# A third exact block in Q's projection, with the engines' orders around it rearranged, in a decoder layer on one core

## The chip, the cores and the metric

One core of one Trainium2 chip runs the whole program. The metric is device time of one execution, in microseconds. Both kernels are timed on the same chip.

## The reference

Three blocks follow each other on x of 2 x 512 rows and 1024 columns, each with a LayerNorm in front and a residual sum behind:

```python
x = x + attn(layernorm(x), q_codes, q_scales, ...)   # 32 heads of 128, 8 K/V heads, rotary, causal
x = x + matmul(fake_quant(layernorm(x)), fake_quant(ctx))   # ctx 2 x 1024 x 1024, codes 0..255
x = x + einsum('bsi,oi->bso', layernorm(x), bw)      # bw = mean|w| * sign(w) - clip(w) + clip(w)
```

The attention's four weight matrices are 4-bit codes with a float scale for each 128 input rows and each output column:

```python
w = codes.astype(float32) - 8.0
w = w * repeat(scales, 128, axis=0)
q = hidden @ w_q        # 1024 x 4096; K and V 1024 x 1024; O 4096 x 1024
```

## The kernel before

**Products.** A float32 product is made of float16 halves: upper by upper, upper by lower and lower by upper, three matmuls of TensorE (`three_products`). Where a factor is a code it is exact in float16, and two matmuls do.

**Slots.** After LayerNorm, V and K, the attention runs over 64 slots (p = 0 to 63). A slot is one head h and one batch b: eight groups g of eight slots i, h = i // 2, b = i % 2. Groups 1 to 4 (slots 8 to 39) are a hardware loop and also handle the cross attention's context (`with_ctx`). Slots 0 to 6 and 40 to 63 carry units of the feed-forward weight: an early part (clip, sign, difference, sum) and a late part (upper and lower half, turned by DMA). Work of several tiles overlaps in a slot p: scores and softmax of p, the weighing of V (`weigh`) of p - 1, the O projection of earlier heads in four units (`o_unit`, `o_add`), and Q of p + 2 (`Q_AHEAD`).

**Q.** Q^T of a tile has eight blocks of 128 input rows. From the fifth tile on (`by_parts`) the first `N_EXACT` = 2 of them use the codes themselves. `q_exact(0)` multiplies block 0, two matmuls, into the bank `q_ps`; ScalarE then multiplies the bank by the ratio of the scales of blocks 0 and 1 (`q_base(0)`, L1313); `q_exact(1)` adds block 1; `q_base(1)` brings the sum to block 1's scale; `q_part` adds the other six blocks by three products each, with weights whose scale was multiplied in beforehand. The ratios are computed once in seven small steps on VectorE (`ratio_step`), one in each of the K phase's rounds x = 4 to 10, and put into columns of `o_table`.

**Pieces.** Weights arrive in pieces of 512 columns, one a slot. VectorE multiplies codes by scales (`piece_scale`, L1894), ScalarE writes the upper half (`piece`, L1215, L1216), VectorE the lower (`piece_lo`, L1900). In even slots the first 256 columns of a piece are exact ones: ScalarE copies the codes, VectorE skips them. In odd slots all 512 are scaled.

**Rotation.** ScalarE copies the finished Q (`q_copy`) and swaps its halves (`q_swap`), GpSimd multiplies by cosine and sine (`q_turn`, `sine`), VectorE adds (`q_sum`, L2054), ScalarE writes the upper half (`q_hi`, L1321), GpSimd the lower (`q_lo`, L1707).

**Softmax.** The scores' 128-row blocks come in three units, `SCORE_UNITS = [[(3, 0)], [(2, 0), (0, 384)], [(1, 0)]]`: widths 512; 384 and 128; 256. VectorE takes the maxima (`maxima`, L2141), ScalarE the exponentials with their sums (`exps`, L1346), VectorE the reciprocals (L2224 for units 0 and 1, L2232 for unit 2), GpSimd normalises (`norm`, L1687), ScalarE and GpSimd split into halves (L1373, L1694), DMA turns them, TensorE weighs (`weigh`, L949) into the bank `pv_ps`, the second of `side_ps`. `ao_part` (ScalarE) and `ao_rest` (VectorE) split that.

**Order.** Every engine's order in a slot is written by hand in its `slot` function, with semaphores between engines. TensorE's is: scores 0, `q_exact(0)`, O unit 3 of the slot before, scores 1, `q_exact(1)`, O unit 0, scores 2, `q_part`, O units 1 and 2, weigh. A bank of O is free when VectorE's `o_add` of the unit two before is done.

**Feed-forward unit.** GpSimd clips 128x256 weights (`wf_clip`), ScalarE takes the sign (`wf_sign`, L1408), VectorE forms mean times sign less clipped (`wf_difference`, L2101), GpSimd adds the clipped again (`wf_add`); one slot later ScalarE and VectorE split into halves (L1415, `wf_lower` L2107).

## Time and profile before

| | |
|---|---|
| median of 3 runs | 1050.31 us (1050.2 to 1050.74) |
| the profiled execution | 1050.22 us, span 1048.4 us |
| TensorE, VectorE, ScalarE, GpSimd busy in the span | 97%, 86%, 74%, 75% |
| granted TensorE clock | 1.00 |
| distance from one slot's start to the next, slots 8 to 61 | 11.46 us |

The span is from the first to the last instruction. Busy time counts an instruction's whole record, and on TensorE records of neighbouring matmuls overlap, so 100% there says that matmuls follow each other without a gap. In a timeline each line is one instruction or several like ones: its start, its length, its engine and source line, and in brackets how long the engine stood idle before it and what ended that. A slot starts with the first 512-column matmul of the scores.

### The profile page before, as it was taken

Reading aid. Unit: us, or ns where it says so; the run is one execution under the profiler, and the core shown is the slowest. Engines: PE = TensorE matmul, PEld = TensorE weight load, DVE = VectorE, ACT = ScalarE, POOL = GpSimd, SP = SyncE. Lnnn points to the kernel's source line nnn. Section 1 sums busy time; section 2 is a strip of 40 time slices with the busy share of each in tenths; the row PEclk is TensorE's granted clock in tenths of the full one; section 3 lists DMA queues with packets and bytes.
Section 4 is the critical chain, followed back from the end, with each engine's and each line's share of the span. In section 5 each row is a group of like instructions: output and inputs, shape, how many; then the busy total and the mean of one; then the engine's idle time right before and its main releaser. Section 6 shows DMA issues by size and latency. Waiting matters only on the chain.

```text
span 1048.4 us, 18487 instructions
## 1 busy us (share of the span) xinstructions
PE 1015.7 (97%) x5296; PEld 500.5 (48%) x5296; DVE 902.7 (86%) x1651; ACT 774.4 (74%) x1712; POOL 788.9 (75%) x833
## 2 busy tenths in 40 slices
PE   5999998999999999999999999999999999989998
PEld 3444343445555555555555455545555554454443
DVE  7989997699888888888888889999999998887773
ACT  5547766888898888888888888888888887473210
POOL 3678787899878887887888789999999999332200
PEclk9999999999999999999999999999999999999999
DMA  9783301676887676667667766777787765534442
GB/s 337 258 199 121 116 26 34 145 152 157 161 162 166 138 165 158 147 152 159 165 138 165 157 147 140 153 165 150 156 150 156 160 138 113 118 122 96 88 96 74
DMA packets 309804, 152.01 MB, mean 145 GB/s; under 512 B 257728, under 2 KB 274240, under 8 KB 309728
## 3 DMA queue, kind: packets, MB, share of 16 engines
q1 hardware_dynamic: 301952, 137.76, 58.0%
q10 hardware_dynamic: 7776, 13.37, 4.5%
q8 instruction: 31, 0.51, 0.2%
q14 instruction: 45, 0.37, 0.1%
HBM read 85.26 MB, written 4.19 MB: 85 GB/s over the span
## 4 chain that ended last, share of the span: by engine, by line
PE 82%; DVE 6%; POOL 5%; ACT 3%; issue 2%; DMA 1%; ACTq 0%; SPq 0%; DVEq 0%; POOLq 0%
PE out_ps L969 10%; PE proj_ps L969 9%; PE side_ps L949 9%; PE side_ps L757 8%; PE side_ps L759 8%; PE side_ps L758 8%; PE side_ps L845 5%; PE proj_ps L1130 5%; PE score_ps L932 3%; PE score_ps L933 3%; PE score_ps L934 3%; PE proj_ps L1135 2%; PE score_ps L1100 2%; PE out_ps L780 1%; PE proj_ps L757 1%
## 5 line engine op out<-in xcount | busy, mean ns | idle before, releaser
L1687 POOL TENSOR_SCALAR prob<-prob,row_inv 128x512 f32<-128x512 f32 (+3 forms) x256 | 196.7, 779 | 81.9 <-DVE row_inv L2224 80.3
L1694 POOL TENSOR_TENSOR w_b<-prob,w_b 128x896 f16<-128x896 f32 (+2 forms) x192 | 186.0, 995 | 6.5 <-ACT w_b L1373 6.4
L1346 ACT ACTIVATE prob<-score_ps,neg_max 128x512 f32<-128x512 f32 (+3 forms) x256 | 132.9, 526 | 30.7 <-DVE neg_max L2141 29.1
L2154 DVE SCALAR_TENSOR_TENSOR x_acc<-out_ps,o_now,x_acc 128x1024 f32<-128x1024 f32 x120 | 153.1, 1276 | 1.3 <-PE out_ps L969 1.3
L2154 DVE SCALAR_TENSOR_TENSOR x_acc<-proj_ps,o_now,x_acc 128x1024 f32<-128x1024 f32 x120 | 153.0, 1275 | 0.0
L757 PE MATMUL side_ps<-hT,w_a 128*128 128x512 f16 x384 | 145.5, 379 | 0.5 <-ACT side_ps L1313 0.2
L759 PE MATMUL side_ps<-hT,w_a 128*128 128x512 f16 x384 | 145.5, 379 | 0.0
L758 PE MATMUL side_ps<-hT,w_a 128*128 128x512 f16 x384 | 145.5, 379 | 0.0
L2141 DVE CUSTOM_DVE_ANT_0 score_ps<-score_ps,mask_b 128x512 f32<-128x512 f32 (+3 forms) x256 | 122.7, 501 | 16.9 <-PE score_ps L934 16.6
L969 PE MATMUL proj_ps<-work,w_b 128*128 128x512 f16 x496 | 127.3, 379 | 1.9 <-DVE x_acc L2154 1.5
L969 PE MATMUL out_ps<-work,w_b 128*128 128x512 f16 x496 | 127.3, 379 | 0.8 <-DVE x_acc L2154 0.7
L949 PE MATMUL side_ps<-work,v_sb 128*128 128x512 f16 (+3 forms) x768 | 114.8, 299 | 0.2 <-DMA work<-w_b 0.2
L1900 DVE SCALAR_TENSOR_TENSOR w_a<-stage_s,w_a 128x256 f16<-128x256 f32 (+1 forms) x64 | 64.7, 1010 | 43.4 <-ACT w_a L1216 43.1
L1373 ACT ACTIVATE w_b<-prob 128x896 f16<-128x896 f32 (+2 forms) x192 | 99.3, 550 | 3.6 <-POOL prob L1687 1.6
L1313 ACT ACTIVATE side_ps<-side_ps,o_now 128x512 f32<-128x512 f32 x120 | 79.3, 661 | 27.8 <-PE side_ps L845 24.3
L1682 POOL TENSOR_TENSOR swapped<-swapped,sin_t 128x512 f32<-128x512 f32 x77 | 99.7, 1295 | 0.0
L949 PEld LDWEIGHTS side_ps<-work,v_sb 128*128 128x128 f16 (+1 forms) x768 | 69.6, 98 | 45.3 <-DMA work<-w_b 1.2
L932 PE MATMUL score_ps<-k_sb,q_sb 128*128 (+4 forms) x256 | 76.7, 299 | 3.6 <-ACT prob L1346 2.0
L1707 POOL TENSOR_TENSOR q_sb<-rot,q_sb 128x512 f16<-128x512 f32 x62 | 78.9, 1273 | 0.0
L969 PEld LDWEIGHTS proj_ps<-work,w_b 128*128 128x128 f16 x496 | 48.2, 98 | 60.2 <-DVE x_acc L2154 2.5
L969 PEld LDWEIGHTS out_ps<-work,w_b 128*128 128x128 f16 x496 | 48.3, 98 | 59.7 <-DVE x_acc L2154 2.0
L933 PE MATMUL score_ps<-k_sb,q_sb 128*128 (+4 forms) x256 | 76.6, 299 | 0.0
(276 smaller groups left out, 2230.1 us busy)
## 6 DMA issues: line engine op xcount, KB each, us to landing
stage_c<-in_codes_dram SPq DMA_DIRECT2D x72, 256.0 KB, 2.9
stage_o<-in_codes_dram SPq DMA_DIRECT2D x64, 256.0 KB, 3.3
stage_s<-in_scales_dram SPq DMA_DIRECT2D x34, 256.0 KB, 3.7
ctx_raw<-in_ctx_dram ACTq DMA_DIRECT2D x32, 256.0 KB, 3.2
work<-w_b SPq DMA_TRANSPOSE x261, 3.1
x_acc<-in_x_dram SPq DMA_DIRECT2D x8, 512.0 KB, 8.9
k_sb<-in_codes_dram SPq DMA_DIRECT2D x16, 256.0 KB, 7.0
v_sb<-in_scales_dram SPq DMA_DIRECT2D x16, 256.0 KB, 7.4
```

The lines of the kernel that those rows point to most:

```text
L757: pe.matmul(o, stat(0), mov(0), start=first, stop=False, skip_group_check=onto)
L758: pe.matmul(o, stat(0), mov(1), start=False, stop=False, skip_group_check=onto)
L759: return pe.matmul(o, stat(1), mov(0), start=False, stop=last, skip_group_check=onto)
L932: pe.matmul(o, q[0], k[0], start=True, stop=False)
L933: pe.matmul(o, q[0], k[1], start=False, stop=False)
L949: mm = pe.matmul(pv_ps[:, kb * P:S], v_sb[:, bass.ds(g, 1), l, b * TB + kb, :].rearrange("p a d -> p (a d)"), probT[:, m, at:kb + (TB - 1) ...
L969: mm = pe.matmul(o[:, b, :], o_codes[:, h % RING, cb * P:(cb + 1) * P], ao[:, h % 2, l, b * S:(b + 1) * S], start=l == 0, stop=l == 1)
L1346: ins = act.activation(prob[:, SCORE_AT[qb]:SCORE_AT[qb] + w], score_ps[:, score_bank(i, u), off:off + w], ACT.Exp, bias=neg_max[:, c:c + ...
L1687: return pool.tensor_scalar(prob[:, at:at + w], prob[:, at:at + w], row_inv[:, col:col + 1], P_UP, ALU.mult, ALU.mult)
L1694: ins = pool.tensor_tensor(prob16[:, 1, to:to + w], prob[:, at:at + w], prob16[:, 0, to:to + w], ALU.subtract)
L2141: ins = dve.tensor_tensor_reduce(s, s, mask_b[:, S - w:S], -1.0, MAX_FROM, ALU.add, ALU.min, neg_max[:, c:c + 1])
L2154: ins = dve.scalar_tensor_tensor(y, u, s, y, ALU.mult, ALU.add)
```

## The change

`N_EXACT` goes from 2 to 3. What goes with it:

- TensorE: `q_exact(2)`, two matmuls, stands for the third block's three. The unit of scores with two blocks is cut in two parts; `q_exact(1)` comes between them, `q_exact(2)` behind O unit 0, and O unit 1 moves ahead of scores 2.
- ScalarE: `q_base(1)` moves ahead of the first exponentials, `q_base(2)` is new behind them, O's codes are cut behind it, Q's upper half moves ahead of the third exponentials. The second conversion of the context's codes (128x512, 8-bit codes to bfloat16) leaves ScalarE for VectorE. K's late swap and upper half move to the ends of slots 1 and 2.
- VectorE: Q's sum moves ahead of the third maxima. O's first add stands ahead of that sum in slots without context and behind the first reciprocal in slots with context, where the conversion follows the second reciprocal. The late K steps move behind the feed-forward difference. In even slots `piece_scale` and `piece_lo` skip 384 columns, not 256.
- The ratios take ten steps and not seven; `q_ratio` has two rows per head and lies in the end of `ctx_raw`.
- For feed-forward units 8 to 29 the sign goes to `pv_ps` and the difference reads it there. ScalarE waits for the attention output of two slots before to have left the bank, and `weigh` waits for the difference.

```diff
-N_EXACT = 2
+N_EXACT = 3
+RATIO_STEPS = 3 * N_EXACT + 1
+        def in_psum(u):
+            return KB <= u < WF_UNITS - 2
+        def wf_sign_place(u):
+            return pv_ps[:, 0:WF_W] if in_psum(u) else wf_place(u)[1]
# TensorE, weigh
                 pe.wait_ge(prob_turned, p * TURNED + TURNED)
+                if known(p) and WF_FROM <= p + 1 and in_psum(wf_early(p + 1) or 0):
+                    pe.wait_ge(wf_diff, wf_early(p + 1) + 1)
# TensorE, slot
-                first_o = known(p) and p == O_LAG
-                if has_o and not first_o:
+                if known(p) and p == O_LAG:
+                    o_unit(p, i, 0)
+                elif has_o:
                     o_unit(p - 1, prev[1], 3)
-                scores(p, i, g, 1)
-                if first_o:
-                    o_unit(p, i, 0)
-                    o_unit(p, i, 1)
+                scores(p, i, g, 1, slice(0, 1))
                 if has_ahead and parts:
                     q_exact(*ahead, 1)
+                scores(p, i, g, 1, slice(1, 2))
...
-                if has_o and not first_o:
-                    o_unit(p, i, 0)
+                if has_o:
+                    o_unit(p, i, int(known(p) and p == O_LAG))
+                if has_ahead and parts:
+                    q_exact(*ahead, 2)
                 if has_ahead and not parts:
                     q_part(*ahead, range(0, 1))
+                if has_o and not (known(p) and p == O_LAG):
+                    o_unit(p, i, 1)
                 scores(p, i, g, 2)
...
-                    if not first_o:
-                        o_unit(p, i, 1)
                     o_unit(p, i, 2)
# ScalarE, wf_sign
-                if u >= 2:
+                if in_psum(u):
+                    act.wait_ge(ao_ready, WF_FROM + u - KB - 1)
+                elif u >= 2:
                     act.wait_ge(wf_split, u)
-                act.activation(diff, raw, ACT.Sign).then_inc(wf_signed, 1)
+                act.activation(wf_sign_place(u), wf_place(u)[0], ACT.Sign).then_inc(wf_signed, 1)
# ScalarE, slot
                     q_base(*next_q, 0)
-                if known(p) and p == 1:
-                    late_swaps()
-                if known(p) and p == 2:
-                    late_upper()
+                if has_ahead and by_parts(p + Q_AHEAD):
+                    q_base(*next_q, 1)
                 exps(p, i, 0)
                 if has_ahead and by_parts(p + Q_AHEAD):
-                    q_base(*next_q, 1)
+                    q_base(*next_q, 2)
+                o_cut(p, i)
                 if has_next and not by_parts(p + 1):
                     q_hi(p + 1)
-                o_cut(p, i)
                 exps(p, i, 1)
+                if has_next and by_parts(p + 1):
+                    q_hi(p + 1)
...
                 exps(p, i, 2)
+                if known(p) and p == 1:
+                    late_swaps()
+                if known(p) and p == 2:
+                    late_upper()
...
-                if has_next and by_parts(p + 1):
-                    q_hi(p + 1)
-                if with_ctx:
-                    act.wait_ge(ctx_scaled, q + 1)
-                    act.activation(dst, ctx_codes, ACT.Copy, bias=-Q_MID).then_inc(ctx_free, 1)
# VectorE, slot
                 maxima(p, i, 1)
+                if not with_ctx:
+                    first_add()
+                if has_next and by_parts(p + 1):
+                    q_sum(p + 1)
                 maxima(p, i, 2)
-                if has_o:
-                    if i % B:
-                        dve.wait_ge(o_now_ready, g * RF + i // B)
-                    o_add(p, i, 0)
                 dve.wait_ge(exp_done, p * 3 + 2)
                 dve.reciprocal(row_inv[:, 0:3], row_sum[:, 0:3]).then_inc(inv_ready[0], 1)
-                if has_next and by_parts(p + 1):
-                    q_sum(p + 1)
+                if with_ctx:
+                    first_add()
...
                 dve.reciprocal(row_inv[:, 3:4], row_sum[:, 3:4]).then_inc(inv_ready[1], 1)
+                if with_ctx:
+                    q, dst = ctx_half(g, i)
+                    dve.wait_ge(ctx_scaled, q + 1)
+                    dve.tensor_scalar(dst, ctx_codes, Q_MID, None, ALU.subtract).then_inc(ctx_free, 1)
```

## Rows read from the trace of the kernel before

**Rows 1.** The page: busy us, share of the span, instructions.

```profile
PE 1015.7 (97%) x5296; PEld 500.5 (48%) x5296; DVE 902.7 (86%) x1651; ACT 774.4 (74%) x1712; POOL 788.9 (75%) x833
```

**Rows 2.** Stretches: length, busy PE, PEld, DVE, ACT, POOL, clock, DMA share, GB/s.

```profile
400.00:500.00 100.00, 100.00 (x541) 50.59 (x540) 84.34 (x160) 88.28 (x203) 82.47 (x88) 1.00 0.69 157
...
700.00:800.00 100.00, 100.00 (x541) 50.57 (x539) 96.71 (x178) 85.07 (x203) 95.13 (x106) 1.00 0.76 157
```

**Rows 3.** Waits of TensorE from 210 to 880 us.

```profile
PE score_ps L932 <- POOL q_sb L1707: 0.2, 1, 0.2
```

**Rows 4.** Timeline of TensorE, an odd slot with context and the next.

```profile
502.87 0.38 PE L932 MATMUL score_ps<-k_sb,q_sb 128*128 x1
...
512.70 1.79 PE L949 MATMUL side_ps<-work,v_sb 128*128 128x512 f16 x12
514.33 0.38 PE L932 MATMUL score_ps<-k_sb,q_sb 128*128 x1
...
518.55 0.38 PE L757 MATMUL side_ps<-hT,w_a 128*128 128x512 f16 x1
...
522.43 1.03 PE L969 MATMUL out_ps<-work,w_b 128*128 128x512 f16 x4
```

**Rows 5.** Timeline of ScalarE in that slot.

```profile
504.15 0.66 ACT L1313 ACTIVATE side_ps<-side_ps,o_now 128x512 f32<-128x512 f32 x1 [0.29 <-PE side_ps L845]
505.19 0.69 ACT L1346 ACTIVATE prob<-score_ps,neg_max 128x512 f32<-128x512 f32 x1 [0.37 <-DVE neg_max L2141]
...
510.26 0.61 ACT L1459 ACTIVATE v_sb<-ctx_raw 128x512 bf16<-128x512 uint8 x1
```

**Rows 6.** Timeline of all engines around a step that writes the ratio's table.

```profile
128.38 1.65 POOL L1723 TENSOR_TENSOR x_acc<-x_acc 128x512 f32<-128x512 f32 x1 [0.27 <-DVE x_acc L1918]
...
128.83 1.25 DVE L2090 TENSOR_SCALAR work<-stats 128x29 f32<-128x29 f32 x1
...
129.98 0.15 DVE L2091 TENSOR_SCALAR work<-stats 128x3 f32<-128x3 f32 x1
```

**Rows 7.** Timeline of VectorE in the odd slot from 502.87.

```profile
509.03 0.66 DVE L2054 TENSOR_TENSOR rot<-rot,swapped 128x512 f32<-128x512 f32 x1
509.61 0.68 DVE L1894 SCALAR_TENSOR_TENSOR stage_s<-stage_c,stage_s 128x512 f32<-128x512 int32 x1
...
511.43 1.58 DVE L1900 SCALAR_TENSOR_TENSOR w_a<-stage_s,w_a 128x512 f16<-128x512 f32 x1 [1.06 <-ACT w_a L1216]
```

**Rows 8.** Timeline of VectorE, an odd slot with a feed-forward unit.

```profile
782.48 0.43 DVE L2141 CUSTOM_DVE_ANT_0 score_ps<-score_ps,mask_b 128x256 f32<-128x256 f32 x1 [0.32 <-PE score_ps L934]
...
784.02 0.17 DVE L2224 RECIPROCAL row_inv<-row_sum 128x3 f32<-128x3 f32 x1
...
785.36 0.76 DVE L2107 SCALAR_TENSOR_TENSOR w_b<-w_b 128x256 f16<-128x256 f32 x1
786.07 1.05 DVE L1900 SCALAR_TENSOR_TENSOR w_a<-stage_s,w_a 128x512 f16<-128x512 f32 x1
787.03 1.38 DVE L2101 SCALAR_TENSOR_TENSOR w_b<-w_b,wf_mean 128x256 f32<-128x256 f32 x1
```

**Rows 9.** Timeline of TensorE, the start of that slot.

```profile
777.95 0.38 PE L932 MATMUL score_ps<-k_sb,q_sb 128*128 128x512 f16 x1
```

**Rows 10.** Timeline of ScalarE in that slot, the third exponentials.

```profile
783.49 0.48 ACT L1346 ACTIVATE prob<-score_ps,neg_max 128x256 f32<-128x256 f32 x1
```

**Rows 11.** Timeline of GpSimd, two odd slots with a feed-forward unit.

```profile
692.66 2.22 POOL L1687 TENSOR_SCALAR prob<-prob,row_inv 128x512 f32<-128x512 f32 x2 [0.85 <-DVE row_inv L2224]
...
702.16 1.27 POOL L1682 TENSOR_TENSOR swapped<-swapped,sin_t 128x512 f32<-128x512 f32 x1
...
784.36 2.22 POOL L1687 TENSOR_SCALAR prob<-prob,row_inv 128x512 f32<-128x512 f32 x2 [0.85 <-DVE row_inv L2224]
```

**Rows 12.** Timeline of TensorE at the end of the K phase.

```profile
164.17 1.26 PE L780 MATMUL score_ps<-hT,w_a 128*128 128x512 f16 x4 [1.94 <-DVE x_acc L1918]
```

More of the change, by code:

```diff
@@ L107 @@
 RATIO_FROM = 4
-RATIO_STEPS = 7
 CB = D // P
@@ L921, in scores @@
                         pe.wait_ge(k_rest, K_TILES * K_BY_DVE)
-                    if known(p) and p == O_LAG:
+                    if known(p) and p == SLOTS - 1:
                         pe.wait_ge(k_ready, K_TILES)
                     pe.wait_ge(q_ready, p + 1)
-                if not (known(p) and 3 * p + u < 2):
+                units = SCORE_UNITS[u][part]
+                if units[0] == SCORE_UNITS[u][0] and not (known(p) and 3 * p + u < 2):
                     pe.wait_ge(exp_done, p * 3 + (u - 1))
-                for qb, off in SCORE_UNITS[u]:
+                for qb, off in units:
                     w = (qb + 1) * P
@@ L2081, in ratio_step @@
                 elif k == 2:
-                    ins = dve.tensor_tensor(by, by, rows[:, :, 1], ALU.add)
-                elif k == 3:
-                    ins = dve.reciprocal(per, by)
-                elif k == 4:
-                    ins = dve.tensor_tensor(per, rows[:, :, 0], per, ALU.mult)
-                else:
-                    row, up = ((per, 1.0), (by, Q_UP))[k - 5]
-                    c = CB + k - 5
+                    ins = dve.tensor_tensor(by, by, of, ALU.add)
+                elif k < RATIO_STEPS - 1 and k % 3 == 0:
+                    ins = dve.reciprocal(per, by[:, :, e])
+                elif k < RATIO_STEPS - 1 and k % 3 == 1:
+                    ins = dve.tensor_tensor(per, by[:, :, e - 1] if e else rows[:, :, 0], per, ALU.mult)
+                else:
+                    row, up = (per, 1.0) if k < RATIO_STEPS - 1 else (by[:, :, N_EXACT - 2], Q_UP)
+                    c = CB + e
                     dve.tensor_scalar(o_table[:, 0:NH - Q_LEAD, c], row[:, Q_LEAD:NH], up, None, ALU.mult)
```

41 lines of the change are left out of this document (26 added, 15 removed).

## The prediction

> **What bounds the kernel now.** I read the page's busy shares first: TensorE 97%, VectorE 86%, the others three quarters [rows 1]. The table by stretches says where that holds: in both stretches shown TensorE is busy for 100.00 of 100 us, while VectorE goes from 84 to 97 and GpSimd from 82 to 95 us, ScalarE from 88 to 85 [rows 2]. TensorE's list of waits for 210 to 880 us holds two waits of 0.2 us each; the one shown is one of them [rows 3]. So in the slots the time is the number of columns that TensorE is fed. One slot is 514.33 - 502.87 = 11.46 us; 18 matmuls of 512 columns run from 518.55 to 522.43, 0.2156 us apiece [rows 4]. A slot's matmuls are 4 + 18 for Q, 16 for O, and 3840 columns each in the scores and in the weighing, 53.0 of the 512-column kind: 53 x 0.2156 = 11.43. Nothing but matmuls is in the slot. The granted clock is 1.00 throughout [rows 2], the 2.4 GHz level, so no clock term enters.
>
> **What the change takes from TensorE.** A third block from exact codes needs two products in place of three: one matmul fewer in each slot whose Q is made by parts. Those are Q's tiles 4 to 63, 60 of them, made in slots 2 to 61: 60 x 0.2156 = 12.9 us, if every slot stays TensorE's. A slot would then take 11.24 us. Everything else is the question whether the others keep up with 11.24 us. I write the new slot out by TensorE's columns, from its start at 0: scores of the 512 block to 0.65, first exact pair to 1.08, O unit to 1.94, the 384 block to 2.43, second pair to 2.87, the 128 block to 3.03, O unit to 3.89, third pair to 4.32, O unit to 5.18, the 256 block to 5.51, fifteen Q matmuls to 8.74, O unit to 9.61, weighing to 11.24. A result is there 0.16 later (a matmul of 0.38 issued every 0.2156).
>
> **ScalarE.** It gets a third rescale of Q's bank, 0.66 us [rows 5]. Rescale 1 starts at 1.28 as now (504.15 - 502.87 [rows 5]); the second, now ahead of the first exponentials, waits for the second pair, 2.87 + 0.16 + 0.04 = 3.07, and is done by 3.73, against 3.89 when the third pair wants it. The first exponentials follow from 3.66, 0.7 us plus their sum's reading [rows 5], the third rescale at 4.52, done by 5.18, against 5.51. Both are covered, by 0.16 and 0.33 us: thin. Room is made in the 32 slots with the context (8 to 39): the code conversion of 0.61 us [rows 5] goes to VectorE. ScalarE is busy 88.28 of 100 us now [rows 2], 10.1 per slot, and stays there in these slots (0.66 in, 0.61 out), and has 11.24. The first rescale need only end by 2.43, so it may start 0.5 us later than 1.28 before anything waits. Cost taken: nothing; if that cover is gone, each 0.1 us over is 0.1 us per slot.
>
> **VectorE, slots 8 to 39.** Added: the conversion, 128x512 from 8-bit codes. The trace has none on VectorE; from below it is the 0.15 us of a 3-column instruction of its kind, from above the 0.66 of a two-input 512 [rows 6, 7]; I take 0.5, nearer to the 512-wide one. Removed: 128 columns of the scaling and the rest in every second slot. In the others the late part of the slot now reads: reciprocal 6.6, O's add to 7.9, scaling (0.68 [rows 7]) to 8.5, conversion to 9.0, then the rest. That one takes 1.58 us [rows 7] and runs to about 10.7, then two adds to 13.1, which is 1.9 us into the next slot. There the attention output's rest, the first maxima and O's fourth add follow, to 4.3 or 4.4, and TensorE's O unit at 4.32 needs that add, which it did not before since it stood behind Q's part. I price this at 0.1 us in every second slot: 16 x 0.1 = 1.6 us; bounds 0 and 16 x 0.4 = 6.4.
>
> A reason for the upper bound is in the trace: the same table step of 29 columns takes 1.25 us where the 3-column one takes 0.15 [rows 6], and GpSimd's 1.65 us instruction runs from 128.38 until about its end: a one-input VectorE instruction can stand for over 1 us while GpSimd works. The Trainium skill's page SBUF — State Buffer, section "SBUF: two separate sides", says that the shared port pair is an exclusive lock which VectorE's two-port and two-input instructions and GpSimd's hold for a whole instruction; by that rule the conversion is a new contender, and this case's rows agree as far as they go. That rule is the third rival below.
>
> **The signs, slots 40 to 61.** Two effects. The difference (VectorE) now reads the sign from the bank: today it takes 1.38 us for 256 columns, and the maxima over 256 columns of a bank take 0.43 [rows 8]. It gets 0.95 us shorter. Against it, the weighing now has to wait for the difference, because both use one bank. TensorE begins to weigh at 512.70 - 502.87 = 9.83 now [rows 4] and at 9.61 then; the difference now ends at 787.03 + 1.38 - 777.95 = 10.46 [rows 8, 9]. New time of it, in a slot with a full piece: the last exponentials, at 783.49 now, 5.54 into the slot [rows 9, 10], move behind the third rescale and Q's upper half and start near 7.4; so the second reciprocal is at 8.0, the unit's lower half (0.76, from 8.0) to 8.75, the piece's rest (1.05) to 9.7, the difference (0.4) to 10.1 [rows 8]. Stall 0.5; if the two before it run undisturbed (0.4 and 0.7) it is near 0. I take 0.35 in each of the 11 full slots; in the 11 others the rest covers 128 columns and the difference ends near 9.5, no stall. 11 x 0.35 = 3.9 us; bounds 0 and 11 x 0.8 + 11 x 0.3 = 12.1.
>
> **Q's sum ahead of the third maxima.** It takes 0.66 us [rows 7] off the stretch in which GpSimd normalises, and puts GpSimd into a ring: sine done, sum, maxima, reciprocal, GpSimd's normalising, and round to the sine. From its start at 692.66 to the sine's end at 702.16 + 1.27 it is 10.77 us in a slot with a full piece [rows 11]. With sum 0.66, maxima 0.43 and 784.36 - 784.02 = 0.34 to the start [rows 7, 8, 11] that would be 12.2, over 11.24. I don't take it for the bound: the sum itself no longer delays the normalising (0.6 of the 10.77), and the difference's clash (I take 0.3 of it) is gone: 9.9 + 1.4 = 11.3 in these slots, less in those between, which have 128 columns for 512. It is cover of nearly nothing, so a rival.
>
> **The start.** The ratio needs three more steps, of which one is a table write like the 1.25 us one [rows 6]; around 156 us it falls where VectorE is what TensorE waits for (1.94 us at 164.17 [rows 12]). I take 0.5 us lost, bounds -0.3 and 1.5. Slots 2 to 7 also have the feed-forward units, and three rescales in a row where ScalarE is behind; I count their gain as nothing, 6 x 0.2156 = 1.3 us given up, bounds 0 and 2.5. Moving the late K work to the ends of slots 1 and 2 I cost at nothing: K's last tile is wanted in slot 7 only, five slots later.
>
> **Queues.** No DMA is added or moved. The conversion frees the context's buffer at 9.0 to 10 and the next load is issued at the next slot's start, as now; O's codes are cut some 1.3 us later than now, and the next load behind that cut is wanted a slot later. Behind the weighing's new wait TensorE's queue holds the next slot's scores, so a stall there moves the whole next slot, all engines alike, and is lost in full.
>
> **Sum.** 12.9 - 1.6 - 3.9 - 0.5 - 1.3 = 5.6 us. The profiled execution took 1050.22 with a span of 1048.4; the median is 1050.31. So 1050.3 - 5.6 = 1044.7.
>
> **Rivals.**
> 1. The forecast: part of the matmul's time is given back. 1041.5 to 1048. Chance 0.44.
> 2. All covers hold: the whole matmul, 12.9 less 0.5 at the start, 1037.9 (to 1041). For it: VectorE and ScalarE stand idle for 12 to 16 of 100 us in the slots up to 39 [rows 2], and the difference gets shorter. Against: covers of 0.1 to 0.3 us. 0.22.
> 3. The conversion contends with GpSimd: it or the rest behind it is pushed by one GpSimd instruction, 0.45 us of stall in every second slot instead of 0.1. 16 x 0.35 = 5.6 more: 1050.3, no change. 0.12.
> 4. The weighing waits in every late slot. It decides from the point where the 22 slots stall by 9.5 / 22 = 0.43 us on average; at its upper bound the change costs 12.1 - 3.9 = 8.2 more: 1052.9, slower. For it: the difference ends 0.6 us after the weighing's start today. Against: it is 0.95 shorter. 0.12.
> 5. The ring: late slots at 11.7 us instead of 11.24 + 0.18, so 22 x 0.28 = 6.2 more, 1050.9. For it: the 12.2 above. 0.10.
>
> **Range and chances.** Cases 1 and 2 and most of 3 to 5 lie between 1037.5 and 1052; case 1's own range is 1041.5 to 1048. About 0.2%, 2 us, is what a measurement tells from none. Faster: 0.41 of case 1, all of 2, 0.05 of the rest: 0.68. Same: 0.03 of case 1, 0.09 of case 3, 0.02 of 4 and 5: 0.14. Slower: what is left, 0.18.
>
> **What would show it.** Q's products by three fall from 18 to 15 a slot. Slots of 8 to 39 take 11.24 to 11.3 us; a wait on VectorE's add before the O unit ahead of the 256 block means case 3. In slots 40 to 61 a wait of the weighing on the difference, in every second slot, of 0.2 to 0.6 us; waits of the 512 block on q_sb (GpSimd) mean the ring. The wait at 164 us grows by less than 1.5. I am wrong if the second or third pair waits for a rescale in every slot: ScalarE would then be the bound.

## The result and the profile after

The changed kernel takes 1055.05 us (median of 5 runs, 1054.95 to 1055.44) against 1050.61 us (5 runs, 1050.20 to 1050.84) of the kernel before beside it: ratio 1.0044, 95% interval 1.0033 to 1.0055. It is slower by 4.4 us where 5.6 us less were forecast. The profiled span is 1053.2 us, 4.8 more than before.

The changed kernel's page, part 1 (answers to [rows 1]):

```profile
PE 1010.7 (96%) x5236; PEld 489.3 (46%) x5236; DVE 909.0 (86%) x1688; ACT 786.2 (75%) x1740; POOL 761.5 (72%) x833
```

The 60 matmuls are gone (5296 to 5236), and TensorE is busy 5 us less, not 13 (a busy span covers short gaps too). The stretches, as [rows 2]:

```profile
400.00:500.00 100.00, 99.99 (x534) 49.16 (x533) 91.37 (x171) 89.07 (x205) 81.39 (x89) 1.00 0.69 158
700.00:800.00 100.00, 97.13 (x519) 47.92 (x518) 89.03 (x174) 87.09 (x209) 86.04 (x102) 1.00 0.71 150
```

In the first, TensorE executes 534 matmuls in 100 us where it executed 541; always fed, it executes 543 to 545 in this order (s9 below). In the second it is 519, and the column of busy time shows 2.9 us of idleness. The clock is 1.00 in both. TensorE's list of waits, 210 to 880 us (answers to [rows 3]):

```profile
PE side_ps L959 <- issue: 6.0, 10, 0.7
PE side_ps L851 <- ACT side_ps L1324: 0.7, 2, 0.3
...
```

L959 is the weighing; its 6.0 us stand under "issue", a wait for which the view names no releaser. The list counts idle time from the end of the record before, which is 0.16 us longer than the distance between matmuls, so it shows 0.64 where 0.80 is lost and leaves the short waits out. Slot by slot, with a slot measured from the first matmul of its 512 block to the next one's:

| stretch | before, us | after, us | change | if only the matmuls went | lost |
|---|---|---|---|---|---|
| first instruction to slot 0 | 167.66 | 166.73 | -0.93 | 0 | -0.9 |
| slots 0 and 1 | 23.93 | 24.29 | +0.36 | 0 | 0.4 |
| slots 2 to 7 | 70.58 | 71.69 | +1.11 | -1.29 | 2.4 |
| slots 8 to 39 (with context) | 366.78 | 363.76 | -3.02 | -6.90 | 3.9 |
| slots 40 to 61 | 252.15 | 257.41 | +5.26 | -4.74 | 10.0 |
| slot 62, slot 63 to the end | 167.30 | 169.32 | +2.02 | 0 | 2.0 |

The sum of the changes is 4.80, the difference of the spans. Before, every slot from 5 to 61 took 11.46. After, odd slots with the context take 11.24 and even ones 11.51 (slot 8: 11.25); slots 42 to 59 take 12.04 if even and 11.48 if odd. Slot 40 takes 11.51 and slot 41 11.67. Slots 60 and 61 take 11.24: their signs are in the bank too, but no piece is left to scale and split there.

**A late even slot.** Timeline of all engines of the changed kernel in the slot that TensorE begins at 814.33 (columns as in [rows 6]):

```profile
814.33 0.38 PE L939 MATMUL score_ps<-k_sb,q_sb 128*128 128x512 f16 x1
...
821.56 1.25 POOL L1698 TENSOR_SCALAR prob<-prob,row_inv 128x512 f32<-128x512 f32 x2 [1.14 <-DVE row_inv L2246]
...
822.50 0.58 DVE L2122 SCALAR_TENSOR_TENSOR w_b<-w_b 128x256 f16<-128x256 f32 x1
...
822.78 1.32 POOL L1718 TENSOR_TENSOR q_sb<-rot,q_sb 128x512 f16<-128x512 f32 x1
...
822.90 0.37 ACT L1420 ACTIVATE side_ps<-w_b 128x256 f32<-128x256 f32 x1
823.03 1.21 DVE L1911 SCALAR_TENSOR_TENSOR w_a<-stage_s,w_a 128x128 f16<-128x128 f32 x1
...
824.17 0.47 DVE L2115 SCALAR_TENSOR_TENSOR w_b<-side_ps,wf_mean,w_b 128x256 f32<-128x256 f32 x1
...
824.74 0.38 PE L959 MATMUL side_ps<-work,v_sb 128*128 128x512 f16 x1 [0.64 <-issue]
826.37 0.38 PE L939 MATMUL score_ps<-k_sb,q_sb 128*128 128x512 f16 x1
```

The sign is there at 823.27, but VectorE's queue has the rest of the piece ahead of the difference. That rest covers 128 columns only and takes 1.21 us. It starts 0.25 after GpSimd's lower half of Q (822.78 + 1.32 = 824.10) and ends at 824.24, 0.14 behind it. The difference follows, 0.47 us, and the weighing begins at 824.74, 10.41 into the slot where 9.61 was to be had: 0.80 lost. In an even late slot of the kernel before, which TensorE began at 789.41, the order of the two was the other way round (timelines of VectorE and GpSimd):

```profile
797.54 0.50 DVE L1900 SCALAR_TENSOR_TENSOR w_a<-stage_s,w_a 128x256 f16<-128x256 f32 x1 [0.23 <-ACT w_a L1216]
797.74 1.32 POOL L1707 TENSOR_TENSOR q_sb<-rot,q_sb 128x512 f16<-128x512 f32 x1
```

The rest began 8.13 into the slot and GpSimd's lower half of Q at 8.33; after the change they begin at 8.70 and 8.45 (within 0.02 in all nine slots; before, within 0.1). So VectorE came 0.6 later, behind the later third exponentials, while GpSimd came only 0.1 later: its normalising starts later too, but takes 1.25 us where an even slot took 1.95 before. In the odd slot behind it (VectorE's timeline):

```profile
834.41 0.40 DVE L2122 SCALAR_TENSOR_TENSOR w_b<-w_b 128x256 f16<-128x256 f32 x1
834.85 0.87 DVE L1911 SCALAR_TENSOR_TENSOR w_a<-stage_s,w_a 128x512 f16<-128x512 f32 x1
835.65 0.47 DVE L2115 SCALAR_TENSOR_TENSOR w_b<-side_ps,wf_mean,w_b 128x256 f32<-128x256 f32 x1
```

Four times the columns in 0.87 us; the weighing begins at 836.22, 9.85 into its slot, 0.24 late.

**An even slot with the context** (TensorE begins it at 558.22). Timeline of all engines around the end of the slot before, and TensorE's second exact pair in it:

```profile
553.86 1.28 DVE L2169 SCALAR_TENSOR_TENSOR x_acc<-proj_ps,o_now,x_acc 128x1024 f32<-128x1024 f32 x1
...
555.05 0.73 DVE L1905 SCALAR_TENSOR_TENSOR stage_s<-stage_c,stage_s 128x512 f32<-128x512 int32 x1
...
555.22 1.59 POOL L1718 TENSOR_TENSOR q_sb<-rot,q_sb 128x512 f16<-128x512 f32 x1
...
555.78 1.30 DVE L2258 TENSOR_SCALAR k_sb<-ctx_raw 128x512 uint8 x1
555.82 0.63 ACT L1227 ACTIVATE w_a<-stage_s 128x512 f16<-128x512 f32 x1 [0.53 <-DVE stage_s L1905]
...
560.82 0.60 PE L851 MATMUL side_ps<-hT,w_a 128*128 128x512 f16 x2
```

ScalarE waits 0.53 us at its cut of the piece for VectorE's scaling, which stands behind O's first add. Everything behind the cut is late, the first rescale too (1.89 into the slot, not 1.28), and TensorE's second pair starts 2.60 into the slot, not 2.43. The conversion takes 1.30 us, behind GpSimd again, and stands ahead of O's adds; the O unit ahead of the 256 block starts 0.07 to 0.09 late.

### The profile page after: what moved, and what is told of

Read it like the earlier page. It is cut to its first block, busy times and chain, and to the rows that moved or that the text cites. A ratio compares the mean times of both kernels' runs of the same rounds, so it can differ in the third digit from the quotient of the medians.

```text
span 1053.2 us, 18594 instructions
## 1 busy us (share of the span) xinstructions
PE 1010.7 (96%) x5236; PEld 489.3 (46%) x5236; DVE 909.0 (86%) x1688; ACT 786.2 (75%) x1740; POOL 761.5 (72%) x833
## 4 chain that ended last, share of the span: by engine, by line
PE 77%; DVE 7%; POOL 6%; issue 5%; ACT 3%; DMA 1%; ACTq 0%; SPq 0%; DVEq 0%; POOLq 0%
PE out_ps L979 9%; PE side_ps L959 9%; PE proj_ps L979 9%; PE side_ps L851 7%; PE side_ps L765 6%; PE side_ps L763 6%; PE side_ps L764 6%; PE proj_ps L1141 5%; PE score_ps L939 3%; PE score_ps L941 3%; PE score_ps L940 3%; PE proj_ps L1146 2%; PE score_ps L1111 2%; POOL w_b L1705 2%; PE proj_ps L763 1%
## 5 line engine op out<-in xcount | busy, mean ns | idle before, releaser
L1698 POOL TENSOR_SCALAR prob<-prob,row_inv 128x512 f32<-128x512 f32 (+3 forms) x256 | 159.6, 635 | 111.2 <-DVE row_inv L2246 108.5
L1324 ACT ACTIVATE side_ps<-side_ps,o_now 128x512 f32<-128x512 f32 x180 | 118.9, 661 | 63.0 <-PE side_ps L851 56.8
L763 PE MATMUL side_ps<-hT,w_a 128*128 128x512 f16 x324 | 122.8, 379 | 0.6 <-ACT side_ps L1324 0.6
L765 PE MATMUL side_ps<-hT,w_a 128*128 128x512 f16 x324 | 122.8, 379 | 0.0
L764 PE MATMUL side_ps<-hT,w_a 128*128 128x512 f16 x324 | 122.8, 379 | 0.0
L959 PE MATMUL side_ps<-work,v_sb 128*128 128x512 f16 (+3 forms) x768 | 114.7, 299 | 6.8 <-issue 6.0
L851 PE MATMUL side_ps<-hT,w_a 128*128 128x512 f16 x360 | 107.3, 380 | 2.0 <-ACT side_ps L1324 1.9
L959 PEld LDWEIGHTS side_ps<-work,v_sb 128*128 128x128 f16 (+1 forms) x768 | 68.3, 98 | 56.0 <-issue 15.5
L1718 POOL TENSOR_TENSOR q_sb<-rot,q_sb 128x512 f16<-128x512 f32 x62 | 87.0, 1404 | 0.9 <-ACT q_sb L1332 0.9
L939 PE MATMUL score_ps<-k_sb,q_sb 128*128 (+4 forms) x256 | 76.6, 299 | 4.3 <-ACT prob L1357 2.2
L940 PE MATMUL score_ps<-k_sb,q_sb 128*128 (+4 forms) x256 | 76.6, 299 | 0.0
L941 PE MATMUL score_ps<-k_sb,q_sb 128*128 (+4 forms) x256 | 76.4, 299 | 0.0
```

The costliest lines, as they stand in the source:

```text
L763: pe.matmul(o, stat(0), mov(0), start=first, stop=False, skip_group_check=onto)
L764: pe.matmul(o, stat(0), mov(1), start=False, stop=False, skip_group_check=onto)
L765: return pe.matmul(o, stat(1), mov(0), start=False, stop=last, skip_group_check=onto)
L851: mm = pe.matmul(q_ps, w_a[:, 0, w:w + P], hT[:, l, e, i % B * S:(i % B + 1) * S], start=l + e == 0, stop=l == 1, skip_group_check=e > 0)
L959: mm = pe.matmul(pv_ps[:, kb * P:S], v_sb[:, bass.ds(g, 1), l, b * TB + kb, :].rearrange("p a d -> p (a d)"), probT[:, m, at:kb + (TB - 1) ...
L1324: act.activation(q_ps, q_ps, ACT.Copy, scale=o_now[:, (i // B + 1) % 2, CB + e:CB + e + 1])\
```

## The experiments

Each is an edit of the changed kernel, measured beside the kernel before (1050.3 to 1051.3 us in the three sets). A difference to the changed kernel is therefore one between sets, good to about 1 us; where less is at stake, the slots' lengths in the traces decide. The expectations stand as written before the runs; the diffs are cut, and a remark behind # in them is mine.

### s1_signs_sbuf: the signs back in SBUF

```diff
         def in_psum(u):
-            return KB <= u < WF_UNITS - 2
+            return False
```

> The changed kernel with one part undone: the signs of all feed-forward units stay in SBUF, so the weighing waits for no difference. The changed kernel's slots 42 to 59 alternate between 12.05 and 11.48 us, before the change all were 11.46. Theory A (the weighing waits for the difference, because they share a bank): the wait is gone; if nothing else is late the 18 slots fall to 11.24 us, 9.5 us in all, 1045.5. VectorE gets 0.9 us per slot back to do (1.38 in place of 0.47), so it may be the one that is full; then 11.4 to 11.5 and 1049 to 1050. Rival B (the ring sine, Q's sum, maxima, reciprocal, GpSimd): the slots stay at 11.7 or above, 1054 to 1056, and the idle of TensorE is ahead of the scores, on q_sb.

Measured: 1053.07 us (ratio 1.0019, 1.0010 to 1.0029), 2.0 less than the changed kernel. The weighing's wait is gone from the list; another has come:

```profile
PE side_ps L851 <- ACT side_ps L1324: 4.1, 12, 0.4
```

Late slots take 11.52 even and 11.77 odd. The rest of the piece still takes 1.22 us in even slots, and ScalarE's sign now waits for VectorE's lower half in the same place, so that ScalarE is late for the second pair in the odd slot; in the even one an O unit waits 0.27 for VectorE's add. The bank removed that wait and put the weighing in its place; by itself, in this order, it costs about 2 us (2.0 by the medians, 1.5 by the profiled spans, 1053.2 and 1051.7), almost all of it in slots 40 to 61, which take 255.4 us for 257.4. Neither place of the signs brings the forecast time, so the bank is not the cause by itself.

### s2_diff_first: the sign and the difference ahead of the piece

```diff
+                if sign_first:              # units with their sign in the bank
+                    wf_sign(wf_early(p))
                 if has_piece:
                     q_cut(p, i)
...
+                if diff_first:
+                    wf_difference(wf_early(p))
                 if has_piece:
                     piece_lo(n, i % 2, q_region(i), Q_UP, (EXACT, 0)[i % B])
```

> The changed kernel with two orders altered for units 8 to 29: ScalarE takes the sign ahead of cutting Q's piece, and VectorE forms the difference ahead of the piece's lower half. Bank and waits are the changed kernel's. Theory A2 (the difference is late because it stands behind the lower half, which in even slots waits for GpSimd's q_lo: 1.21 us for 128 columns): the difference ends near 9.1 us into the slot, before the weighing at 9.61, slots 42 to 59 take 11.24 to 11.3, 1045.5 to 1046.5. Rival: the difference itself is what is slow, or the sign: then stalls stay over 0.3 us and the time is over 1050. Slots 8 to 39 stay at 11.51 and 11.24.

Measured: 1048.02 us (0.9971, 0.9960 to 0.9983), 7.0 less than the changed kernel and 0.3% faster than the one before. Late slots take 11.49 to 11.58 even and 11.24 odd. The same instructions on VectorE and the reciprocal ahead of them, even slot:

```profile
771.33 0.16 DVE L2257 RECIPROCAL row_inv<-row_sum 128x1 f32<-128x1 f32 x1 [0.85 <-ACT prob L1357]
771.41 0.58 DVE L2125 SCALAR_TENSOR_TENSOR w_b<-w_b 128x256 f16<-128x256 f32 x1
772.11 0.48 DVE L2118 SCALAR_TENSOR_TENSOR w_b<-side_ps,wf_mean,w_b 128x256 f32<-128x256 f32 x1
772.51 0.65 DVE L1914 SCALAR_TENSOR_TENSOR w_a<-stage_s,w_a 128x128 f16<-128x128 f32 x1
```

The rest of the piece is behind the difference, where nobody on the path waits for it. Of the 10.0 us lost in the late slots 6.5 hung on this order (slots 40 to 61 take 250.9 us for 257.4). The edit moves the sign on ScalarE as well; but in the changed kernel the sign was there at 823.27, while VectorE was busy with the rest until 824.24. The forecast end of the difference, 9.1, is missed in even slots: with the stalls gone the second reciprocal comes later in the slot (8.58 for 8.10 in slot 54), the difference ends at 9.84, and 0.34 stay.

### s3_scale_first: in slots with the context, the scaling ahead of O's first add

```diff
-                if with_ctx:
-                    first_add()
                 if has_piece:
                     piece_scale(n, i % 2, (EXACT, 0)[i % B])
+                if with_ctx:
+                    first_add()
```

> The changed kernel with one order altered in slots 8 to 39: VectorE scales the piece ahead of O's first add, not behind it. In the changed kernel every even slot is 0.27 us longer: the second exact pair waits 0.17 us for the first rescale, the O unit ahead of scores 2 waits 0.09 for O's add. Theory C: ScalarE is late because its cut of the piece stands idle 0.53 us for the scaling, behind O's first add; with the scaling first the 0.17 go and 16 x 0.17 = 2.7 us are saved, 1052.3. Rival: VectorE as a whole is late (its conversion takes 1.24 to 1.30 us behind GpSimd's q_lo) and the wait only moves: under 1 us saved, over 1054.

Measured: 1050.67 us (0.9993, 0.9984 to 1.0003), 4.4 less than the changed kernel. All slots from 8 to 39 take 11.24 to 11.25, the late ones are as they were. The conversion still takes 1.21 to 1.35 us in this kernel:

```profile
541.24 1.22 DVE L2258 TENSOR_SCALAR k_sb<-ctx_raw 128x512 uint8 x1
```

So it was not the conversion's length that TensorE waited for, but the order in which VectorE came to the scaling.

### s4_ounit_back: O's unit 1 behind Q's part, as before the change

```diff
-                if has_o and not (known(p) and p == O_LAG):
-                    o_unit(p, i, 1)
                 scores(p, i, g, 2)
...
                 if has_o:
+                    if not (known(p) and p == O_LAG):
+                        o_unit(p, i, 1)
                     o_unit(p, i, 2)
```

> The changed kernel with one order of TensorE undone: O unit 1 stands behind Q's part again. Theory D (it is the cover of the third rescale): scores 2 ends at 4.65 us and Q's part must wait for the rescale, which ends near 5.2: 0.5 us more in each of some 58 slots except where they stalled at the end of the slot anyway, 1070 to 1085. Rival: the third rescale comes early enough by then and the O unit's own wait of 0.09 us goes: 1053 to 1054.

Measured: 1075.85 us (1.0236, 1.0219 to 1.0253). Slots take 11.85 in the middle and 11.92 late. TensorE at the first of Q's products by three:

```profile
506.02 0.39 PE L763 MATMUL side_ps<-hT,w_a 128*128 128x512 f16 x1 [0.27 <-ACT side_ps L1324]
```

The O unit's 0.86 us are what covers the third rescale. The forecast had 0.33 us to spare there; without the unit every slot takes 0.6 to 0.7 us more than the 11.24 of its matmuls.

### s5_three_edits: s2, s3, and slot 62's O unit back

```diff
-                if has_o and not (known(p) and p == O_LAG):
+                if has_o and has_ahead and not (known(p) and p == O_LAG):
                     o_unit(p, i, 1)
                 scores(p, i, g, 2)
+                if has_o and not has_ahead:
+                    o_unit(p, i, 1)
```

> Three edits of order at once on the changed kernel: the sign and the difference ahead of the piece's cut and rest (alone 7.0 us less), the scaling ahead of O's first add in the slots with the context (alone 4.4 us less), and in slot 62 O's unit 1 behind the 256 block as before the change (that slot takes 9.03 us so in the kernel where it was moved back everywhere, against 9.80). If each loss is local to its slots they add up: 1055.05 - 7.0 - 4.4 - 0.8 = 1042.9 us, slots 8 to 39 at 11.24, even late slots at 11.5. Rival: the same slack is counted twice, the slots that no longer wait push the next engine, and it comes to 1045 or more.

Measured: 1044.38 us (0.9940, 0.9924 to 0.9957). s2's and s3's gains add up to within 0.7, 1055.05 - 7.0 - 4.4 = 1043.7; the third edit gave nothing (slot 62 still takes 9.79). It took 9.03 in s4, where the slots ahead of it were longer; that this gave VectorE the time to catch up was not tested.

### s6_conv_scalare: the conversion on ScalarE again

```diff
                 if has_piece:
                     q_cut(p, i)
+                if with_ctx:
+                    act.wait_ge(ctx_scaled, q + 1)
+                    act.activation(dst, ctx_codes, ACT.Copy, bias=-Q_MID).then_inc(ctx_free, 1)
```

(and VectorE's conversion removed)

> The changed kernel with one edit undone: the conversion of the context's codes is done by ScalarE again, behind the cut of the piece, not by VectorE. If VectorE's conversion (1.24 to 1.30 us behind GpSimd's lower half of Q) is what makes even slots 8 to 39 take 11.51 instead of 11.24, they fall to 11.24 and the time goes to 1055.05 - 4.3 = 1050.7. Rival: the conversion had to leave ScalarE, since ScalarE with three rescales has 10.7 us of work in 11.24: then a rescale comes late in every slot with the context, slots of 11.4 to 11.7 in both parities, 1055 to 1063 us.

Measured: 1070.24 us (1.0186, 1.0169 to 1.0203): the rival, and worse. Slots with the context take 12.01 even and 11.63 odd (slot 13: 12.76), and TensorE's list for 262 to 640 us has one entry:

```profile
PE side_ps L851 <- ACT side_ps L1324: 12.2, 31, 1.3
```

The conversion's move is worth (0.50 + 0.39) x 16 = 14.2 us. My theory that it was the loss in these slots fell here and in s3.

### s7_sum_late: Q's sum and upper half back where they were

```diff
-                if has_next and by_parts(p + 1):
-                    q_sum(p + 1)
                 maxima(p, i, 2)
                 dve.wait_ge(exp_done, p * 3 + 2)
                 dve.reciprocal(row_inv[:, 0:3], row_sum[:, 0:3]).then_inc(inv_ready[0], 1)
+                if has_next and by_parts(p + 1):
+                    q_sum(p + 1)
```

(and ScalarE's upper half of Q behind the third exponentials)

> The changed kernel with Q's sum back behind the first reciprocal and Q's upper half back behind the third exponentials. Theory: the sum's new place made GpSimd's normalising short (1.25 us for 2.22) and so brought its lower half of Q onto VectorE's rest of the piece; with the sum back that rest of 128 columns falls from 1.21 to about 0.3 in even late slots, the weighing waits 0.3 or less instead of 0.81, and the time falls by 11 x 0.5 or more, to 1049.5 or less, also in even slots 8 to 39. Rival one: the collision only moves, since the lower half then runs later, on the conversion or the difference: 1055. Rival two: the sum's new place is needed to bring Q's halves in time: the 512 block waits for Q in every slot, 1058 or more.

Measured: 1096.87 us (1.0442, 1.0424 to 1.0459). Both halves of the theory show, in different slots. Late even slots fall from 12.04 to 11.27; two engines in one of them, GpSimd and VectorE:

```profile
840.80 1.86 POOL L1698 TENSOR_SCALAR prob<-prob,row_inv 128x512 f32<-128x512 f32 x2 [0.94 <-DVE row_inv L2244]
842.63 1.25 POOL L1718 TENSOR_TENSOR q_sb<-rot,q_sb 128x512 f16<-128x512 f32 x1
```

```profile
842.56 0.29 DVE L1911 SCALAR_TENSOR_TENSOR w_a<-stage_s,w_a 128x128 f16<-128x128 f32 x1 [0.36 <-ACT w_a L1227]
842.84 0.48 DVE L2115 SCALAR_TENSOR_TENSOR w_b<-side_ps,wf_mean,w_b 128x256 f32<-128x256 f32 x1
```

The normalising is slow again, the lower half of Q starts 0.07 after the rest of the piece instead of 0.25 ahead of it, and the same 128 columns take 0.29 us. Late odd slots rise from 11.48 to 11.94. Slots 9 to 40 take 45 us more than in the changed kernel, mostly 12.94 even and 12.56 odd. ScalarE, GpSimd and VectorE in an even one:

```profile
551.39 1.15 POOL L1718 TENSOR_TENSOR q_sb<-rot,q_sb 128x512 f16<-128x512 f32 x1
551.42 1.27 DVE L1905 SCALAR_TENSOR_TENSOR stage_s<-stage_c,stage_s 128x128 f32<-128x128 int32 x1
...
552.73 0.52 ACT L1226 ACTIVATE w_a<-stage_c 128x384 f16<-128x384 int32 x1 [1.58 <-DVE stage_s L1905]
```

Reciprocal, sum, O's add and scaling stand in a row on VectorE, and ScalarE's cut waits 1.58 us for the scaling: s3's mechanism enlarged. And rival one is true here: the collision has moved onto the scaling, which starts 0.03 behind GpSimd's lower half of Q and takes 1.27 us for 128 columns; in s3 the same 128 columns took 0.29. How much of the 45 us each of the two makes was not isolated.

### s8_two_exact: two exact blocks, all else as after

```diff
-N_EXACT = 3
+N_EXACT = 2
```

(and the third pair and the third rescale removed)

> The changed kernel with two blocks from exact codes instead of three, all other edits kept: one matmul more in 60 slots, one rescale of 0.66 us less on ScalarE. By columns alone it would be 1055.05 + 12.9 = 1068.0. Theory: TensorE's saved matmul is given back by waits, so that its removal costs far less: in slots 8 to 39 11.46 to 11.51 for 11.38 on average (+3 to +4), in late slots the stall of the weighing shrinks by the 0.22 that its start moves (11.5 odd, 12.0 even, as now: 0), together 1055 to 1060. The rival is 1065 or more: the new order's stalls are there on top of whatever TensorE has.

Measured: 1069.81 us (1.0183, 1.0166 to 1.0200): the rival. The third block brings 14.8 us in this arrangement, more than its 12.9. TensorE's timeline of a slot with the context shows why:

```profile
489.94 1.03 PE L979 MATMUL proj_ps<-work,w_b 128*128 128x512 f16 x4
491.06 1.04 PE L979 MATMUL out_ps<-work,w_b 128*128 128x512 f16 x4
```

Four matmuls last 0.86, so the second unit could start at 490.80; it waits 0.26 for O's add, in a gap that the third pair fills. Slots of 8 to 39 take 11.72, late ones 12.15 and 11.46. In the late ones the matmul alone brought nearly nothing (12.04 and 11.48 with it): an odd one is at the length of its matmuls with two exact blocks (11.46) and at that of the weighing's wait with three, an even one waits in both.

### s9_diff_earliest: s2 and s3, and the unit's halves earlier

```diff
                 exps(p, i, 1)
+                if upper_first:             # late slots
+                    wf_upper(wf_late(p))
                 if has_next and by_parts(p + 1):
                     q_hi(p + 1)
...
+                if lower_first:             # behind the first reciprocal
+                    wf_lower(wf_late(p))
                 if has_piece:
                     piece_scale(n, i % 2, (EXACT, 0)[i % B])
```

> The two edits of order that paid (the sign and the difference ahead of the piece; the scaling ahead of O's first add in slots with the context), and in slots 41 to 61 also the feed-forward unit's upper half ahead of Q's upper half (ScalarE) and its lower half ahead of the piece's scaling (VectorE), so that the difference stands right behind the second reciprocal. With the two edits alone even late slots take 11.57 us, the weighing waiting 0.26 to 0.33 for the difference. Theory: what is left of the wait is the lower half between the reciprocal and the difference (0.58 us); it goes, even slots fall to 11.24 to 11.3, and the time to 1044.4 - 3.3 = 1041.1 us. Rival: ScalarE's third exponentials come 0.4 later because the upper half now stands ahead of Q's upper half and them; then the reciprocals and the difference come as much later, even and odd slots stay at 11.5 or rise, 1044 to 1050.

Measured: 1041.14 us (0.9914, 0.9896 to 0.9931), 13.9 less than the changed kernel and 9.2 less than the kernel before beside it (1050.29). Every slot from 8 to 61 takes 11.24 to 11.31. The stretches, as [rows 2]:

```profile
400.00:500.00 100.00, 100.00 (x545) 50.69 (x543) 90.06 (x170) 90.40 (x208) 81.48 (x91) 1.00 0.69 154
700.00:800.00 100.00, 100.00 (x543) 49.99 (x542) 92.28 (x181) 89.27 (x215) 89.72 (x107) 1.00 0.75 155
```

and VectorE in an even late slot:

```profile
765.87 0.48 DVE L2121 SCALAR_TENSOR_TENSOR w_b<-side_ps,wf_mean,w_b 128x256 f32<-128x256 f32 x1
766.50 1.18 DVE L1917 SCALAR_TENSOR_TENSOR w_a<-stage_s,w_a 128x128 f16<-128x128 f32 x1 [0.15 <-ACT w_a L1227]
```

The slow rest of 128 columns is back, 1.18 us, and costs nothing: the difference stands ahead of it and is done 0.46 before the weighing begins at 766.81.

### s10_sum_62: and in slot 62 Q's sum ahead of O's add

```diff
-                if not with_ctx:
+                if not with_ctx and has_ahead:
                     first_add()
                 if has_next and by_parts(p + 1):
                     q_sum(p + 1)
+                if not with_ctx and not has_ahead:
+                    first_add()
```

> The kernel of the run beside it (two edits of order and the earlier halves), and in slot 62 Q's sum ahead of O's first add. In the changed kernel slots 62 and 63 are 2.0 us worse than before: slot 62 is 0.73 longer, and slot 63's 512 block waits 1.1 us for Q where it waited 0.4. If that wait is the sum's place behind a 1.28 us add, 0.7 us come back: 1040.4. Rival: O's add comes 0.7 later instead and TensorE's next O unit waits for it in the same measure: 1041.1, no change.

Measured: 1042.19 us (0.9924, 0.9906 to 0.9941), 1.1 more. The rival's wait came, larger than it said:

```profile
877.66 1.87 PE L979 MATMUL proj_ps<-work,w_b 128*128 128x512 f16 x4 [2.00 <-DVE x_acc L2175]
```

The granted clock fell behind it, as the stretches show (columns as in [rows 2]):

```profile
879.00:881.00 2.00, 2.00 (x7) 0.78 (x6) 1.46 (x3) 1.34 (x2) 2.00 (x3) 0.50 0.25 56
875.00:880.00 5.00, 3.00 (x11) 1.10 (x10) 3.35 (x9) 3.28 (x10) 2.67 (x5) 0.77 0.58 118
```

It is 0.50 from 879 to 881, the 1.2 GHz level, and the four matmuls behind the wait take 1.87 us where they took 1.04 in s9, the weighing 2.69 for 1.80. Slot 62 takes 11.71 us for 9.80 and slot 63's 512 block no longer waits; behind that block's start 1.0 us comes back (158.35 us to the end for 159.39). So the edit does help slot 63, and loses more in slot 62, by the wait and the clock together. The base of the expectation was off besides: slot 63's wait for Q is only 0.2 us in s9.

### s11_sum_even: Q's sum late in the late even slots alone

```diff
+                sum_late = known(p) and i % B == 0 and in_psum(wf_early(p) or 0)
-                if has_next and by_parts(p + 1):
+                if has_next and by_parts(p + 1) and not sum_late:
                     q_sum(p + 1)
...
                 dve.reciprocal(row_inv[:, 0:3], row_sum[:, 0:3]).then_inc(inv_ready[0], 1)
+                if sum_late:
+                    q_sum(p + 1)
```

(and ScalarE's upper half of Q likewise)

> The changed kernel with Q's sum behind the first reciprocal, and Q's upper half behind the third exponentials, in the 11 late slots with an even number and nowhere else. With the sum late in all slots those even slots took 11.27 (rest of 128 columns 0.29 us, GpSimd's lower half of Q starting only behind it), the odd ones 11.94. Theory: the collision of a slot is set by the order in that slot, so that it is 11.27 even and 11.48 odd here: 1055.05 - 11 x 0.77 = 1046.6 us. Rival: what a slot gains is handed on, GpSimd and ScalarE come as much later into the odd slot, 11.27 and 11.94 as with the sum late everywhere: 1055.05 - 3.4 = 1051.6.

Measured: 1049.36 us (0.9991, 0.9982 to 1.0001), between the two: slots 42 to 58 even 11.27 as forecast, 43 to 59 odd 11.63, where 11.48 and 11.94 had been expected. Slot 40, which carries the edit too, gets longer, 12.26 for 11.51. So the collision belongs to its slot, but a third of the odd slots' loss in s7 is handed on from the even ones.

### s12_late_k: the late K work back in its places

```diff
-                if known(p) and p == 0:
-                    late_join()
+                if known(p) and p < 3:
+                    (late_join, late_sum, late_lower)[p]()
```

(and ScalarE's `late_swaps`, `late_upper` ahead of the first exponentials)

> The changed kernel with the late K work back in the places that it had in slots 1 and 2 (swaps and upper half ahead of the first exponentials, sum and lower half behind the first reciprocal). Slots 2 to 7 took 1.1 us more after the change although a matmul went. Theory: the loss there is three rescales and Q's sum in slots 4 to 7, not the K work: slots 1 to 3 within 0.2 of now, 1055.05 +- 0.5. Rival: the late K work at the end of slots 1 and 2 delays the conversions behind it and costs the 0.8 us that slots 2 and 3 gained in length: 1054.2 or less. Third: it was moved because it would hold the rescales now: slots 2 and 3 grow by 1 or more, 1056 or more.

Measured: 1054.55 us (1.0041, 1.0026 to 1.0056), the same as the changed kernel. Slot 2 takes 12.23 for 11.87, more than the 0.2 allowed, slot 3 12.90 for 12.92. The K work is not the early loss.

## Why the prediction was wrong, step by step

**TensorE: right.** 60 matmuls, 15 for 18 in Q's products by three. The slot as written out by columns stands in the trace wherever nothing waits (pairs at 0.65, 2.43 and 3.89, weighing at 9.61, length 11.24), and in s9 all 54 slots from 8 to 61 are within 0.07 of it. The gain of 12.9 us was there to be had.

**ScalarE: the covers are real.** s4 takes the O unit's cover away (0.6 a slot), s6 puts 0.6 us of work back (0.4 to 0.5 a slot). The step "may start 0.5 us later than 1.28 before anything waits" held, and the price of nothing did not: in even slots with the context the first rescale starts at 1.89.

**Slots 8 to 39: priced 1.6, measured 3.9 lost.** The forecast wait of an O unit on VectorE's add is there, 0.09 us in every second slot for the 0.1 named. What was missed is the other wait in the same slots, 0.17 of the second pair: the text had "O's add to 7.9, scaling (0.68 [rows 7]) to 8.5" and did not ask who waits for the scaling, ScalarE's cut. s3 turns the two around and both waits go, conversion and all. The conversion was taken at 0.5 and took 1.24 to 1.31. That it stands behind GpSimd, the third rival, is so, but its price is not: with the conversion as long as ever, s3 has none of these slots above 11.25.

**Slots 40 to 61: the step that failed.** "In the 11 others the rest covers 128 columns and the difference ends near 9.5, no stall." Those are the slots that stall most: 0.80 us in nine even slots is 7.2, 0.24 in nine odd ones 2.1, and slots 40 and 41 add 0.7 (0.3 of it in slot 40, where not the weighing waits but the second pair and an O unit, as in the slots before): 10.0 in all, for the 3.9 of the sum. The odd slots came out below the 0.35 named. The difference did fall from 1.38 to 0.47 us, and the second reciprocal came at 8.1, where 8.0 was written. What failed is the duration of the rest of the piece: it had been taken for the number of columns, and 128 columns took 1.21 us behind GpSimd's lower half of Q and 0.29 ahead of it (s7). The difference ended at 10.3, not 9.5. The prediction saw that the sum's new place frees the normalising ("no longer delays"), and used it for the ring alone. One instruction further, GpSimd's lower half of Q starts at 8.45; with the sum back, and the normalising at 1.86, it starts at 8.85, just behind the rest of the piece. s11 shows it by slots, s2 by moving the difference out of the rest's way.

The Trainium skill, page SBUF — State Buffer, section "SBUF: two separate sides", says that the port pair which VectorE and GpSimd share is held by whoever starts first for its whole instruction, when VectorE's has two inputs in SBUF and GpSimd's reads SBUF. The rows above agree: 823.03 behind 822.78 ends 0.14 after GpSimd; s7's scaling at 551.42, behind 551.39, ends 0.15 after it; 842.56 ahead of 842.63 takes 0.29; and the difference, which has one input in the bank, takes 0.47 to 0.49 in all 22 slots of the changed kernel.

**Rival 4 is what happened in the main**, at a mean loss of 10.0 / 22 = 0.45 us in the late slots, just above its point of 0.43 (0.52 in the 18 slots from 42 to 59). Alone it would have given 1044.7 + 10.0 - 3.9 = 1050.8, no change. That the time went beyond its 1052.9 is the sum of smaller terms: 2.3 more lost in slots 8 to 39, 1.1 in slots 2 to 7, 2.0 in the last two, less 1.1 at the start. The ring did not close: no 512 block waits for Q up to slot 62.

**Start, early slots, tail.** The three added table steps were priced at a loss of 0.5 and slot 0 begins 0.9 earlier. TensorE's wait at the end of the K phase [rows 12] is 0.23 us now:

```profile
163.24 1.26 PE L786 MATMUL score_ps<-hT,w_a 128*128 128x512 f16 x4 [0.23 <-DVE x_acc L1929]
```

The two kernels with seven steps start slot 0 at 167.66 and 167.80, the twelve with ten steps at 166.48 to 167.32. The steps move VectorE's work against GpSimd's; which pair is decisive was not isolated. Slots 2 to 7 lost 2.4 for 1.3; s7 brings slots 5 and 7 from 11.77 to 11.25 and the six slots down by 1.0, so most of the 1.1 beyond the forecast is the order around Q's sum there, and s12 excludes the K work. The last two slots' 2.0 us were not priced. There are no Q products in slot 62 to cover VectorE. Of the 2.0, 0.7 is at slot 62's end, where slot 63's 512 block waits 1.07 us for Q and waited 0.38 before, and 1.3 is behind that block's start, where an O unit now waits 0.66 for VectorE's add. In s9 the wait for Q is 0.2, and slot 62 still takes 9.80: TensorE waits 0.7 ahead of the weighing instead. s5 and s10 did not mend it. What would is open.

The terms, forecast and measured: matmuls 12.9 and 12.9; slots 8 to 39 -1.6 and -3.9; late slots -3.9 and -10.0; start, with slots 0 and 1, -0.5 and +0.6; slots 2 to 7 -1.3 and -2.4; tail 0 and -2.0. Sum +5.6 and -4.8.

## What to carry to other kernels

When a new wait hangs on a helper engine, write out what stands ahead of the producer in its queue and price each of those at its duration behind GpSimd, not by its columns; if one of them is wanted by nobody soon, put it behind. When one engine's instruction gets shorter, follow its neighbour's queue one instruction further, since that one starts earlier on something else. A change that loses can still hold most of its gain: here the matmul was worth 12.9 us, and three edits of order in the queues of ScalarE and VectorE brought 1055.05 to 1041.14, 9.2 us below the kernel before.

## What was not expected of the hardware

- A VectorE instruction with two inputs in SBUF took 1.21 us for 128 columns and 0.87 for 512 in neighbouring slots; in s7 and the changed kernel the order of starts against a GpSimd instruction, 0.07 us ahead or 0.25 behind, went with 0.29 or 1.21.
- GpSimd's normalising of the same blocks took 1.25, 1.80, 1.86, 1.95 and 2.22 us in different slots and kernels, with different VectorE instructions beside it.
- VectorE's conversion of 128x512 8-bit codes took 1.21 to 1.35 us behind GpSimd's lower half of Q (changed kernel, s3, s9), and 0.52 in all 16 of s7, where GpSimd was normalising 128 columns in the slot looked at.
- A wait of 2.0 us of TensorE in slot 62 (s10) was followed by a granted clock of 0.50, the lower of the two levels (1.2 and 2.4 GHz), from 879 to 881 us; from 882 it was 1.00 again. In s9, where no wait there is over 1.0, it stayed at 1.00.
